# Edge messages of a graph layer: lookups ahead of the last scatter on TensorE, and two DVE operands kept in a PSUM bank

## The reference, cut to what matters

```python
h = (x_flat @ W_gat).reshape(M, 4, 4)               # heads, experts
a_src, a_dst = (h * att_src).sum(-1), (h * att_dst).sum(-1)
e = leaky_relu(a_src[src] + a_dst[dst], 0.2)
ee = exp(e - segment_max(e, dst)[dst])
denom = segment_sum(ee, dst)
agg = segment_sum(h[src] * (ee / denom[dst])[:, :, None], dst) + b_gat
```

## Time and profile before

| | us |
|---|---|
| median of 3 runs (2399.08 to 2400.2) | 2399.8 |
| profiled execution, its own time | 2394.67 |
| span in its profile, first to last instruction | 2392.9 |
| edge loop (`graph_edges`), from its first decode to its last matmuls | 908.5 to 1560.2 |

### The profile page before, as it was taken

One profiled execution on the slowest core, in us unless ns is written; L12 is line 12 of the kernel. 1 busy time (PEld: TensorE's weight loads), 2 busy tenths in 40 slices (PEclk: granted clock), 3 DMA queues, 4 the chain that ended last, 5 costly groups with the idle time before them and its releaser, 6 DMA issues. The chain is left out here.

```text
span 2392.9 us, 34125 instructions
## 1 busy us (share of the span) xinstructions
PE 1734.6 (72%) x10531; PEld 1329.2 (56%) x10531; DVE 1633.5 (68%) x3612; ACT 748.9 (31%) x2069; POOL 736.9 (31%) x541
## 2 busy tenths in 40 slices
PE   0042069999999856767776776729999499849997
PEld 0042047877887655555554554606667466726665
DVE  7999967777777647677767746754445323567777
ACT  3120047766766520100110010014343212324342
POOL 0581022332332106778878777000000000300000
PEclk9999999999999856887888788869999689669999
DMA  7000000000000020000000111000000811000000
GB/s 281 0 2 3 0 12 0 0 0 0 0 0 0 1 12 7 8 8 7 7 7 7 7 8 7 1 18 1 18 18 18 185 31 31 0 18 18 18 18 18
DMA packets 73271, 47.39 MB, mean 20 GB/s; under 512 B 25553, under 2 KB 69378, under 8 KB 72706
## 3 DMA queue, kind: packets, MB, share of 16 engines
q1 hardware_dynamic: 58914, 41.73, 6.8%
q0 software_dynamic: 12288, 3.96, 2.6%
q10 hardware_dynamic: 2016, 1.06, 0.2%
HBM read 33.21 MB, written 13.50 MB: 20 GB/s over the span
## 5 line engine op out<-in xcount | busy, mean ns | idle before, releaser
L1000 POOL DMA_INDIRECT sb_ge_gs<-source_rows,sb_ge_idx x384 | 466.8, 1216 | 126.9 <-issue 116.1
L1242 PE MATMUL acc<-sb_ge_b,sb_ge_ol 128*128 128x320 f32 x768 | 275.7, 510 | 188.5 <-DVE sb_ge_b L1103 188.5
L1566 DVE SCALAR_TENSOR_TENSOR sb_X<-x_py,sb_x_gc,sb_X 128x128 f32 (+1 forms) x768 | 269.4, 351 | 187.2 <-PE x_py L1506 160.8
L1495 PE MATMUL x_pu<-sb_TT,sb_x_w 128*128 (+1 forms) x512 | 248.1, 609 | 78.2 <-PEq L1521 76.2
L1242 PEld LDWEIGHTS acc<-sb_ge_b,sb_ge_ol 128*128 128x128 f32 x768 | 162.6, 223 | 253.2 <-DVE sb_ge_b L1103 191.5
L1506 PEld LDWEIGHTS x_py<-sb_x_w,sb_x_ht 128*128 128x128 f32 x2048 | 248.1, 192 | 60.8 <-issue 39.5
L235 POOL TENSOR_TENSOR sb_bias<-sb_PB,sb_TT 128x1024 f32<-128x1024 f32 x64 | 151.2, 2363 | 337.6 <-DVE sb_logits L262 337.6
L1485 ACT ACTIVATE sb_x_ht<-x_pu,sb_x_b 128x512 f32<-128x512 f32 x256 | 174.4, 687 | 252.4 <-PE x_pu L1495 252.2
L1506 PE MATMUL x_py<-sb_x_w,sb_x_ht 128*128 128x128 f32 x2048 | 249.6, 275 | 1.3 <-DVE sb_X L1566 1.3
L1013 ACT ACTIVATE sb_ge_olt<-p_turned 128x512 f32<-128x512 f32 x96 | 57.4, 598 | 458.7 <-PE p_turned L1220 450.5
L319 ACT ACTIVATE sb_probs<-sb_logits,sb_neg_max 128x128 f32<-128x128 f32 x512 | 198.4, 390 | 7.0 <-DVE sb_neg_max L273 3.7
(11 more groups left out here) (337 smaller groups left out, 3205.9 us busy)
## 6 DMA issues: line engine op xcount, KB each, us to landing
sb_ge_gs<-source_rows,sb_ge_idx POOLq DMA_INDIRECT x384
sb_z<-in_L_conv_z SPq DMA_DIRECT2D x1, 4096.0 KB, 20.4
sb_TT<-in_L_conv_mask SPq DMA_DIRECT2D x1, 4096.0 KB, 42.8
x_rows<-sb_X SPq DMA_DIRECT2D x4, 1024.0 KB, 5.1
normed_rows<-sb_TT SPq DMA_DIRECT2D x4, 1024.0 KB, 6.5
sb_X<-x_rows SPq DMA_DIRECT2D x2, 2048.0 KB, 20.7
sb_mr_xg<-normed_rows SPq DMA_DIRECT2D x16, 256.0 KB, 3.4
out<-sb_X SPq DMA_DIRECT2D x8, 512.0 KB, 5.3
```

The lines of the kernel that those rows point to most:

```text
L1000: pool.indirect_dma_start(GS[:, j, k, :], None, SRC_T, bass.IndirectOffsetOnAxis(ap=IDX[:, j, k:k + 1], axis=0))\
L1242: last = nc.tensor.matmul(ACC[:, q, 0:WIN * PART], OL[:, j % 2, c * CHUNK + k, :], B[:, c, k, :, :].rearrange("p x w -> p (x w)"), start=F ...
L1495: nc.tensor.matmul(PU[c % 2][:, :], w1[:, c * P:(c + 1) * P], TT[:, ds(g * BANK, BANK)], start=True, stop=True)\
L1566: last = nc.vector.scalar_tensor_tensor(out=xs, in0=PY[(k * YB + b) % NY][:, (e % 4) * C:(e % 4 + 1) * C], scalar=GC[:, u, k * experts + e ...
```

## The change

NUMBERS (the list 0 to 127, now float32) and MSG (the messages of one step) share one PSUM bank, HELD, that TURNED gives up. MSG has one buffer instead of two; the weights go through WT in SBUF and are copied into MSG by DVE. On PE, chunk 0 of the next step is turned ahead of the first scatter, each later turn and lookup comes one chunk earlier, and the last lookup stands before the last scatter.

```diff
-        iota_f = local("iota_f", [P, P])
-        MSG = local("msg", [P, 2, STEP, PART])
+        WT = local("weights", [P, 2, STEP, GHEADS])
-        TURNED = bank("p_turned", [P, 2, BANK])
+        TURNED = bank("p_turned", [P, BANK])
+        HELD = bank("p_held", [P, BANK])
+        NUMBERS = HELD[:, 0:P]
+        MSG = HELD[:, P:P + STEP * PART].rearrange("p (k w) -> p k w", w=PART)
-        AHEAD_T, AHEAD_L = 2, CHUNKS
+        AHEAD_T, AHEAD_L = 1, CHUNKS
...
-                nc.scalar.activation(MSG[:, u, :, GF:], ARG[:, u, :, :], ACT.Exp).then_inc(exped, 1)
+                nc.scalar.activation(WT[:, u, :, :], ARG[:, u, :, :], ACT.Exp).then_inc(exped, 1)
...
-            nc.vector.tensor_copy(iota_f[:, :], iota_i[:, :]).then_inc(iota_cast, 1)
+            nc.vector.tensor_copy(NUMBERS, iota_i[:, :]).then_inc(iota_cast, 1)
...
-                nc.vector.tensor_tensor(OL[:, j % 2, :, :], iota_i[:, :].unsqueeze(1).to_broadcast([P, STEP, P]),
+                nc.vector.tensor_tensor(OL[:, j % 2, :, :], NUMBERS.unsqueeze(1).to_broadcast([P, STEP, P]),
...
                 v.wait_ge(exped, n + 1)
-                nc.vector.tensor_tensor(MSG[:, u, :, 0:GF]...,
+                v.wait_ge(b_made, n * CHUNKS + AHEAD)
+                nc.vector.tensor_copy(MSG[:, :, GF:], WT[:, u, :, :])
+                nc.vector.tensor_tensor(MSG[:, :, 0:GF]...,
                                         GS[:, j, :, 0:GF]...,
-                                        MSG[:, u, :, GF:]..., ALU.mult).then_inc(messages, 1)
+                                        WT[:, u, :, :]..., ALU.mult).then_inc(messages, 1)
...
             def step(t, j, counted, more):
                 n = t * STEPS + j
+                if more:
+                    turn(t, j + 1, 0)
                 for c in range(CHUNKS):
                     scatter(n, j, c)
-                    if more:
-                        turn(t, j + 1, c)
-                        if c > 0:
-                            look(t, j + 1, c - 1)
+                    if more and c < CHUNKS - 1:
+                        turn(t, j + 1, c + 1)
+                        look(t, j + 1, c)
                     if counted is not None:
-                        if c == CHUNKS - 1 and more:
-                            look(t, j + 1, c)
                         count(counted + (j * CPS + c), c % NC)
-                    elif c == CHUNKS - 1 and more:
-                        look(t, j + 1, c)
+                    if more and c == CHUNKS - 2:
+                        look(t, j + 1, c + 1)
```

More of the change, by code:

```diff
@@ L1012, in follow @@
                     act.wait_ge(looked, n * CHUNKS + c + 1)
-                    nc.scalar.activation(OLT[:, c, :], TURNED[:, c % 2, :], ACT.Copy).then_inc(turned_out, 1)
+                    nc.scalar.activation(OLT[:, c, :], TURNED[:, :], ACT.Copy).then_inc(turned_out, 1)
                 act.wait_ge(args, n + 1)
-                nc.scalar.activation(MSG[:, u, :, GF:], ARG[:, u, :, :], ACT.Exp).then_inc(exped, 1)
+                nc.scalar.activation(WT[:, u, :, :], ARG[:, u, :, :], ACT.Exp).then_inc(exped, 1)
             with act.Fori(0, n_both + n_gather + 1) as t:
@@ L1092, in message @@
                 v.wait_ge(exped, n + 1)
-                nc.vector.tensor_tensor(MSG[:, u, :, 0:GF].rearrange("p k (h e) -> p k h e", e=EXPERTS0),
+                v.wait_ge(b_made, n * CHUNKS + AHEAD)
+                nc.vector.tensor_copy(MSG[:, :, GF:], WT[:, u, :, :])
+                nc.vector.tensor_tensor(MSG[:, :, 0:GF].rearrange("p k (h e) -> p k h e", e=EXPERTS0),
                                         GS[:, j, :, 0:GF].rearrange("p k (h e) -> p k h e", e=EXPERTS0),
-                                        MSG[:, u, :, GF:].unsqueeze(3).to_broadcast([P, STEP, GHEADS, EXPERTS0]),
+                                        WT[:, u, :, :].unsqueeze(3).to_broadcast([P, STEP, GHEADS, EXPERTS0]),
                                         ALU.mult).then_inc(messages, 1)
@@ L1103, in block_of @@
                 nc.vector.tensor_tensor(B[:, c, :, :, :], OH[:, j % 2, k, :].unsqueeze(3).to_broadcast(shape),
-                                        MSG[:, j % 2, k, :].unsqueeze(2).to_broadcast(shape), ALU.mult).then_inc(b_made, 1)
+                                        MSG[:, k, :].unsqueeze(2).to_broadcast(shape), ALU.mult).then_inc(b_made, 1)
             def count_bits(at, m):
@@ L1219, in turn @@
                 for k in range(CHUNK):
-                    last = nc.tensor.transpose(TURNED[:, c % 2, k * P:(k + 1) * P], OL[:, j % 2, c * CHUNK + k, :], ident[:, :])
+                    last = nc.tensor.transpose(TURNED[:, k * P:(k + 1) * P], OL[:, j % 2, c * CHUNK + k, :], ident[:, :])
                 last.then_inc(turned, 1)
```

## The result

| | before | after |
|---|---|---|
| median of 4 runs each, us | 2399.6 (2399.1 to 2400.2) | 2340.1 (2336.7 to 2340.7) |
| profiled execution, us | 2394.7 | 2339.8 |
| first block of step 0 to first block of step 23, us | 944.69 to 1541.56: 596.9 | 949.40 to 1487.98: 538.6 |

The ratio is 0.9749, 95% interval 0.9732 to 0.9766: faster by 59.5 us, against 56.3 us forecast (2343.5 us for the median, 2338.4 for the profiled execution). The loop itself lost 58.3 us in 23 steps, 2.53 us a step. The profiled executions differ by 54.8 us. That is less than the loop lost, because the second came later into the loop (its first gather starts at 913.65, before at 909.83), and less than the medians differ, because the execution of before was 5 us under its median.

What follows compares the result with a forecast made beforehand. Bound: PE and DVE handing over once per step, 25.77 us together. 19 counted steps save 47.9 us, four uncounted 9.4, less 1.0 in the prologue: 56.3 us, profiled 2338.4, median 2343.5 us; 8 in 10 range 2323 to 2358.

Steps and rivals of the forecast that it cites:

- The chain's 2.67 us: PE, first scatter to selection: last scatter (2.24 us) and one turn (0.43 us) leave the chain each step.
- l3: PE's last lookup of a step, which releases DVE's selection; moved ahead of the last scatter, forecast to save 2.24 us.
- t0: PE's turn of the next step's first one-hots; moved into PE's idle time before the first scatter, saving 0.43 us.
- Nothing else becomes late: Checks on DVE, counts, one-hots and copies: DVE keeps 3.46 us idle, `one_hots` 1.2 us to spare, uncounted steps wait 0.15.
- s3: PE's last scatter of a step, 2.24 us; moved behind the last lookup, forecast to end about 2.4 us after it.
- The prologue: Before the loop no scatter covers ACT's copy with a single TURNED bank: about 1.0 us lost, once.
- t1: PE's turn of the second chunk's one-hots; in the prologue it waits for the copy of the first, about 1.0 us.
- PSUM operands cost nothing on DVE: DVE operations with an operand in PSUM keep their duration: 0 taken, ends -0.05 and +0.1 us each.
- POOL: Gathers beside OL and the blocks no longer held: POOL's step 19.8 to 22.2 us, under the coming 23.4.
- Rival 2: POOL becomes the bound, its port not freed: 20 us, about half covered by its lead, 10 lost, 2354 us; chance 0.12.
- Rival 1: PE's clock comes back earlier, shortening the first scatter by 0.8 us a step: 18 us more, 2325 us; chance 0.14.
- s0: PE's first scatter of a step, starting the chain; 4.13 us at its start against 2.40 later.

Runs made afterwards that it cites:

- the late counts: The changed kernel with all counts of a step moved behind its last scatter: 2320.8 us, ratio 0.9685 to the kernel before; 0.986 on the first slow chip.

## Why the prediction was right

- *The bound*: a chain with one hand-over each way per step, not a busy engine. Right: with PE's order changed, DVE's wait fell to 110.7 us (about 110 forecast) and the steps followed.
- *The chain's 2.67 us*: PE's part of a step fell by 2.66 us, DVE's rose by 0.13 for a copy put at 0.15. That the loop's sum hit so well (58.3 us, 57.3 forecast) is part luck, since its terms were off in opposite ways. A counted step went from 26.34 to 23.66 us, 2.68 less where 2.52 were forecast (steps of 23.2 to 23.5 were named as the sign); an uncounted one from 24.09 to 22.27, 1.82 less where 2.35 were forecast, and why is open. The shares of the two pieces are less sure than their sum: taken back one by one l3 cost 2.06 us (2.24 forecast) and t0 0.84 (0.43 forecast), together 2.90, more than the 2.66 that both brought at once.
- *Nothing else becomes late*: DVE kept 3.98 us of idle time in the step shown (3.46 forecast). s3 ends 1.45 to 1.59 us before `one_hots` starts (1.2 to spare forecast, 5.9 before the change). PE waits for ACT's copy in no step, not even the 0.15 us put down for the uncounted ones.
- *The prologue*: 1.0 us forecast. t1 idled 0.69 us for the copy, DVE's wait for the counts went from 1.37 to 2.06 us: 0.7.
- *PSUM operands cost nothing on DVE*: OL went from 2284 to 2282 ns, a block from 1484 to 1479. The 62 cycles more that the Trainium skill ("VectorE: DVE Perf Modes", the section on the TRN2 errata) charges for a source in PSUM appear in neither.
- *POOL*: the hold by operations with two SBUF inputs, and its end with one in PSUM, is shown by the four rows of the table and the two stretches below it. POOL's step is now 16 x (1.096 + 0.30) = 22.3 us, where 19.8 to 22.2 were forecast. The Trainium skill ("SBUF — State Buffer", "Who interferes with whom") infers that descriptor generation is not held by a `tensor_tensor`; the gathers of 3.03 us before and 2.44 us after beside such operations disagree. Its rule in the same section, that two SBUF inputs contend with a GpSimd instruction that reads SBUF, agrees with these rows.
- *Rival 2 was the real danger, and its size was off*: 10 us of loss forecast, 18.0 us of loop measured (556.6 - 538.6). The 20 us of it before any cover were about right; the cover was not. The prediction let a lead of some 4 us and the steps that POOL had gained pay for half. The lead was 5.9 us, and DVE began to wait when 1.4 us of it were left after three steps, since a gather takes 2.8 us (median of that run) from issue to landing. So only 4.5 us of lead were there to use.
- *Rival 1 did not happen*: s0 got no shorter, 4.44 us on average against 4.30, and in the step shown it still runs at a granted clock of 0.50. The granted clock from 945 to 1310 us is 0.85 against 0.82, but s0, where the rival looked for its gain, shows nothing of it.

## What to carry to other kernels

When no engine is full, find the instruction that ends the longest wait and move ahead of it only what it depends on; then ask of every engine that ran ahead so far whether its own step is shorter than the new one. A change that is worth nothing alone (here 1.0035) can be a third of the gain once another one makes its engine the bound, so such pairs have to be tried together. In this kernel one operand in PSUM kept VectorE out of GpSimd's way and cost VectorE nothing, and one list of 128 numbers was enough. A gain measured on one chip need not stand on another: time the kernel before on each.

## What was not expected

- The hold moves rather than ends. After the change a gather that starts with the counted one-hots takes up to 2.44 us, over both of them:

```profile
1193.66 0.94 POOL L1002 DMA_INDIRECT sb_ge_gs<-source_rows,sb_ge_idx  x1 [0.30 <-issue]
1194.91 2.44 POOL L1002 DMA_INDIRECT sb_ge_gs<-source_rows,sb_ge_idx  x1 [0.30 <-issue]
```

  Before, gathers came to start with the second of them, and took 1.43:

```profile
947.30 1.43 POOL L1000 DMA_INDIRECT sb_ge_gs<-source_rows,sb_ge_idx  x1 [0.30 <-issue]
```

  So freeing OL and the blocks gave 2.06 us a step (129 ns x 16), not more than OL's hold alone had seemed to be worth.

- On the two chips where all kernels took longer, PE pauses where the profile names nothing that it waited for ("issue"). The timeline of the late counts on the first of them, and of the same kernel on the chip of its second run:

```profile
1025.08 1.40 PE L1255 MATMUL acc<-sb_ge_c_onehot_hi,sb_ge_c_onehot_lo 128*128 128x64 bf16 x41
1027.01 0.19 PE L1255 MATMUL acc<-sb_ge_c_onehot_hi,sb_ge_c_onehot_lo 128*128 128x64 bf16 x1 [0.53 <-issue]
...
1029.89 0.19 PE L1255 MATMUL acc<-sb_ge_c_onehot_hi,sb_ge_c_onehot_lo 128*128 128x64 bf16 x1 [1.23 <-issue]
```
```profile
1168.42 2.10 PE L1255 MATMUL acc<-sb_ge_c_onehot_hi,sb_ge_c_onehot_lo 128*128 128x64 bf16 x64
```

  In this step the pauses are 0.4 to 1.2 us each, and the 64 counts spread over 14 us instead of 2. PE has 179 such pauses in this loop, 220 us in all, and none in the loop on the chip of the second timeline. It is not PE alone: with l3 behind s3 on the first chip PE has 62 such pauses, 142 us, and ACT 15 ahead of its exponential (L1017), 150.8 us. The stages behind the loop took 833 us there as elsewhere. What the engines wait for, why in this loop and why on these chips is open. The kernel before has no trace from them, so its own pauses are not known either.
